# Six dense products of a graph network: tiles written out, transposes one tile ahead, bias added by VectorE

## The reference

```python
h_raw = x @ W.T + b                                   # layer 0, and x @ mag_w.T + mag_b, one column
hidden = x @ Win.T + b_in                             # layer 1
adjustment = jax.nn.relu(hidden @ W1.T + b1) @ W2.T + b2
h = (x @ W).reshape(N, HEADS, HEAD_DIM)               # layer 2, no bias
return x @ m                                          # layer 3, rotations, no bias
```

## Time and profile before

| what | us |
|---|---|
| median of three runs | 10083.64 |
| lowest and highest | 10081.59, 10103.02 |
| the profiled execution's own time | 10127.57 |
| its span, from the first to the last instruction | 10125.8 |
| the six stretches of `project` in it, together | 658.36 |
| mean granted TensorE clock, share of full speed | 0.745 |

### The profile page before, as it was taken

How to read it: one execution, slowest core, us unless ns; L and a number is a source line. 1 busy time by engine, 2 the same in 40 slices (tenths; PEclk the granted TensorE clock), 3 DMA queues, 4 the chain that set the end, 5 groups by cost and what they waited for, 6 DMA issues and landing times. The chain is left out here.

```text
span 10125.8 us, 178077 instructions
## 1 busy us (share of the span) xinstructions
PE 5548.0 (55%) x58295; PEld 4432.9 (44%) x58413; DVE 5392.1 (53%) x12231; ACT 1374.6 (14%) x3130; POOL 4357.0 (43%) x3974
## 2 busy tenths in 40 slices
PE   0001100578775725556677777777767777635552
PEld 0000000467775414333566656666566664323331
DVE  7993000355554434454566645666456663257766
ACT  0000000122211001111112111111011111112210
POOL 6887777200000035530565615656165660046630
PEclk9999555688777555556899988999889996555555
DMA  0000000000000023321555325553255530033320
GB/s 22 3 1 1 1 1 1 0 0 0 0 0 23 2 72 99 99 81 57 159 166 161 98 73 156 166 161 94 79 156 166 161 89 6 5 86 97 97 75 13
DMA packets 707863, 691.02 MB, mean 68 GB/s; under 512 B 234780, under 2 KB 588646, under 8 KB 707456
## 3 DMA queue, kind: packets, MB, share of 16 engines
q0 software_dynamic: 227328, 446.06, 16.5%
q1 hardware_dynamic: 480136, 239.99, 8.5%
HBM read 765.51 MB, written 77.58 MB: 83 GB/s over the span
## 5 line engine op out<-in xcount | busy, mean ns | idle before, releaser
L1632 POOL DMA_INDIRECT kvring<-kvtab,oth x1776 | 1900.9, 1070 | 1421.0 <-issue 711.8
L1001 POOL DMA_INDIRECT e_hg<-htab,oth_d x992 | 993.1, 1001 | 3029.0 <-issue 2597.1
L1683 PE MATMUL ea_pss<-ea_qb,ea_kT 128*128 128x128 f32 x7104 | 1146.0, 297 | 7.9 <-issue 7.6
L1683 PEld LDWEIGHTS ea_pss<-ea_qb,ea_kT 128*128 128x128 f32 x7104 | 1056.7, 213 | 37.8 <-issue 10.6
L1767 DVE TENSOR_REDUCE ea_sc<-ea_pss 128x64 f32<-128x1024 f32 x444 | 543.6, 1224 | 729.5 <-remote 613.1
L1694 PE MATMUL ea_psg<-ea_mix,kvring 128*64 128x64 f32 x14208 | 668.9, 231 | 406.8 <-issue 320.0
L1128 PE MATMUL e_psg<-e_Em,e_hg 128*32 128x32 f32 x15872 | 567.7, 245 | 465.3 <-issue 421.8
L1694 PEld LDWEIGHTS ea_psg<-ea_mix,kvring 128*64 128x64 f32 x14208 | 548.2, 140 | 557.1 <-issue 521.4
L1727 ACT ACTIVATE ea_kT<-ea_pst 128x512 f32<-128x512 f32 x888 | 481.9, 594 | 2260.5 <-remote 1596.5
L1128 PEld LDWEIGHTS e_psg<-e_Em,e_hg 128*32 128x32 f32 x15872 | 435.8, 146 | 634.1 <-issue 539.3
L1680 PE MATMUL ea_pss<-mrow,ea_mk 128*128 128x256 bf16 x1776 | 526.3, 296 | 318.3 <-ACT ea_kT L1727 298.0
(11 more groups left out here) (518 smaller groups left out, 10345.1 us busy)
## 6 DMA issues: line engine op xcount, KB each, us to landing
ea_qb<-qtab SPq DMA_DIRECT2D x1776, 64.0 KB
qtab<-at_qst SPq DMA_DIRECT2D x75, 512.0 KB, 3.3
kvring<-kvtab,oth POOLq DMA_INDIRECT x1776
e_stack<-ohtab SPq DMA_DIRECT2D x744, 32.0 KB
kvtab<-at_kvst SPq DMA_DIRECT2D x75, 256.0 KB, 2.7
e_hg<-htab,oth_d POOLq DMA_INDIRECT x992
ea_mk<-mtab SPq DMA_DIRECT2D x444, 3.0 KB
htab<-Hd SPq DMA_DIRECT2D x2, 3200.0 KB, 11.9
```

Source lines behind the costliest of these rows:

```text
L1001: pool.indirect_dma_start(out=hg[:, b % RING, u, :], out_offset=None, in_=htab, in_offset=bass.IndirectOffsetOnAxis(ap=oth[:, b * 4 + u:b ...
L1632: pool.indirect_dma_start(out=kv[:, b % R, u, :], out_offset=None, in_=kvtab, in_offset=bass.IndirectOffsetOnAxis(ap=oth[:, b * QB + u:b * ...
L1683: mm = pe.matmul(ps_s[r % 2][:, u, k * 2 * HN:(k + 1) * 2 * HN], kT[:, r % 2, u, k, :], qb[:, r, u, :], start=False, stop=True, skip_group ...
```

## The change

`project` is written anew and takes one weight function, one list of targets for a tile, a bias tile of 128 partitions and the function of the copy:

- there is no loop any more; the 25 tiles are written out on each engine;
- `xs` is gone: PE transposes from the source itself;
- PE transposes tile t + 1 before it multiplies tile t; `xT` has three slots, `psx` two, `pso` four;
- the copy from `psx` to `xT` is made by ScalarE (it was VectorE), and VectorE empties `pso` (it was ScalarE);
- the bias matmuls are gone: VectorE adds the bias as it empties `pso`. The bias is loaded as a broadcast to 128 partitions;
- the extra column of `p0` is the 257th column of the same matmul, and VectorE writes it out with a second instruction;
- Relu between `mlp1` and `mlp2` is done by ScalarE when it copies the transposed tiles of `mlp2`, no longer at the end of `mlp1`.

The core of the diff (the old loops, quoted above by the program, are left out):

```diff
-def project(nc, tag, K, src, pieces, store=None, extra=None):
+def project(nc, tag, K, src, w, dst, C=D, bias=None, entry=ACT.Copy):
...
+        xT = ctx.enter_context(nc.sbuf_tensor(f"{tag}_xT", [P, 3, 2, P], F32))
+        ps_x = [ctx.enter_context(nc.psum_tensor(f"{tag}_psx{i}", [P, 2, P], F32)) for i in range(2)]
+        ps_o = [ctx.enter_context(nc.psum_tensor(f"{tag}_pso{i}", [P, 512], F32)) for i in range(4)]
+        with phase(nc, tag, "turn xT mm out") as (block, s):
+            @block.tensor
+            def _(pe):
+                def turn(t):
+                    if t >= 2:
+                        pe.wait_ge(s["xT"], t - 1)
+                    for k in range(2):
+                        tr = pe.transpose(ps_x[t % 2][:, k, :], src[:, t, k * P:(k + 1) * P], K["ident"][:, :])
+                    tr.then_inc(s["turn"], 1)
+
+                turn(0)
+                for t in range(NT):
+                    if t + 1 < NT:
+                        turn(t + 1)
+                    pe.wait_ge(s["xT"], t + 1)
+                    if t >= 4:
+                        pe.wait_ge(s["out"], t - 3)
+                    for k in range(2):
+                        mm = pe.matmul(ps_o[t % 4][:, 0:C], xT[:, t % 3, k, :], w(k), start=(k == 0), stop=(k == 1))
+                    mm.then_inc(s["mm"], 1)
 
             @block.scalar
             def _(act):
...
+                for t in range(NT):
+                    act.wait_ge(s["turn"], t + 1)
+                    if t >= 3:
+                        act.wait_ge(s["mm"], t - 2)
+                    act.activation(xT[:, t % 3], ps_x[t % 2][:, :, :], entry).then_inc(s["xT"], 1)
 
             @block.vector
             def _(dve):
...
+                for t in range(NT):
+                    dve.wait_ge(s["mm"], t + 1)
+                    lo = 0
+                    for here in dst(t):
+                        n = here.shape[-1]
+                        if bias is None:
+                            ins = dve.tensor_copy(here, ps_o[t % 4][:, lo:lo + n])
+                        else:
+                            ins = dve.tensor_tensor(here, ps_o[t % 4][:, lo:lo + n], bias[:, lo:lo + n], ALU.add)
+                        lo += n
+                    ins.then_inc(s["out"], 1)
...
-    with nc.sbuf_tensor(f"{tag}_w", [P, 2, D], F32) as ws, nc.sbuf_tensor(f"{tag}_b", [1, D], F32) as bs:
...
+    with nc.sbuf_tensor(f"{tag}_w", [P, 2, D], F32) as ws, nc.sbuf_tensor(f"{tag}_b", [P, D], F32) as bs:
+        load(nc, tag + "l", [(ws[:, :, :], w.rearrange("(k p) n -> p k n", p=P)), (bs[:, :], b.partition_broadcast(P))])
+        project(nc, tag, K, src, lambda k: ws[:, k, :], lambda t: [dst[:, t, :]], bias=bs, entry=entry)
```

More of the change, by code:

```diff
@@ L1390, in _ @@
             @block.scalar
             def _(act):
[L1392 to L1426, removed]
-                            if bias is not None:
-                                mm = pe.matmul(ps_o[u % 2][q][:, 0:C], K["ones"][0:1, :], bias, start=False, stop=True)
-                            if q == 0 and extra is not None:
-                                mm = pe.matmul(ps_o[u % 2][q][:, 0:C], xT[0:TYPES, u, 2, :], extra, start=False, stop=True)
-                        mm.then_inc(s["mm"], 1)
@@ L1433, in _ @@
+                for t in range(NT):
[3 more added lines that the diff above has]
+                    act.activation(xT[:, t % 3], ps_x[t % 2][:, :, :], entry).then_inc(s["xT"], 1)
             @block.vector
             def _(dve):
-                dve.sem_inc(s["xT"], 1)
-                with dve.Fori(0, NT // U) as i:
-                    for u in range(U):
-                        t = i * U + u
-                        dve.wait_ge(s["turn"], t + U + 1)
-                        if extra is not None:
-                            dve.tensor_copy(xT[0:TYPES, u, 2, :], ps_x[u % 2][0:TYPES, 2, :])
-                        dve.tensor_copy(xT[:, u, 0:2, :], ps_x[u % 2][:, 0:2, :]).then_inc(s["xT"], 1)
@@ L1444, in project @@
-            if store is not None:
-                @block.sync
-                def _(sp):
-                    with sp.Fori(0, NT // U) as i:
-                        for u in range(U):
-                            t = i * U + u
-                            to, slot = store(t, u)
-                            sp.wait_ge(s["out"], t + 3)
-                            sp.dma_start(to, slot).then_inc(st[u], 16)
-                        for u in range(U):
-                            sp.wait_ge(st[u], i * 16 + 16)
-                            sp.sem_inc(s["free"], 1)
+                for t in range(NT):
[9 more added lines that the diff above has]
+                    ins.then_inc(s["out"], 1)
@@ L2175, in program @@
         rows = lambda w: w.rearrange("(k p) n -> p k n", p=P)
-        one = lambda v: v.rearrange("(a n) -> a n", a=1)
         flat = lambda v: v.rearrange("l n -> (l n)")
@@ L2214, in program @@
                     (K["w0"][:, :, 0:D], rows(io["L0_WT"])), (K["w0"][:, :, D:D + 1], io["L0_mag_w"].rearrange("a (k p) -> p k a", p=P)),
-                    (K["b0"][:, 0:D], one(io["L0_b"])), (K["b0"][:, D:D + 1], one(io["L0_mag_b"])),
+                    (K["b0"][:, 0:D], wide(io["L0_b"])), (K["b0"][:, D:D + 1], wide(io["L0_mag_b"])),
                     (K["att0"][:, :, :].rearrange("p a d -> p (a d)"), wide(io["L0_attn_w"].rearrange("a n -> (a n)")))])
```

33 lines of the change are left out of this document (10 added, 23 removed).

## The result

The changed kernel takes 9614.74 us, the median of four executions (9610.43 to 9620.06); the kernel before, beside it on the same chip, 10082.99 (10081.59 to 10103.02). The ratio is 0.9532, with a 95% interval of 0.9520 to 0.9544: 468 us less, where the sum had 474 and the forecast was 9609.

A forecast was written before the change was run, and what follows sets the result against it. Six products run alone between barriers, PE stopping in each tile at half clock. Each becomes 5.5 + 24.15 + 0.69 = 30.3 us; with loads 184.2 instead of 658.4, so 474 off 10083.64 gives 9609 us, range 9573 to 9680.

The forecast's parts named there:

- the sum: Six products and their loads: 184.2 us where they took 658.4, a gain of 474 us.
- the period 1.07: Each tile of the changed products at full clock: 0.21 us of transposes plus 0.86 of matmuls, 1.07 us.
- The stall at the start: Start of each product: first matmuls 1.17 us after the first transposes, of which 0.3 us is a stall.
- The rise, taken at 5.5 us: In each product the granted clock goes from 0.50 to 1.00 after 5.5 us, as in the attention tables.
- a rise after 13 us: Far end for the clock, from the attention update: all products rise after 13 us, 33.8 us per product.
- Slack: Each tile: ScalarE's copy to xT ends about 0.3 us before PE needs it at full clock.
- The swinging clock: Rival, 8 in 100: PE stops briefly in each tile and the clock comes and goes; gain 404, 9680 us.
- each of these has PE stopping in every tile: Argument against the clock never rising: the stretches held at 0.50 had PE stops in every tile.
- The bias matmuls go, 25 x 1.15 = 29 us in each: Four products with bias: 29 us saved in each by taking the bias matmuls off PE.
- the rival that the clock stays low: Rival, 7 in 100: granted clock 0.50 throughout the products, 328 us in all plus 2; 9755 us.
- Code that is fetched too slowly: Rival, 1 in 100: PE waits for written-out code from memory; at 2.5 instructions per us, 10145 us.
- The overlap being absent: Rival, 1 in 100: PE waits for the copy in each tile, 73 us per product, gain 218, 9866 us.

The follow-up runs named there:

- copy_in_4: The changed kernel with ScalarE's copy to xT cut into 4 instructions; 7922.36 us, 8401.79 for the kernel before beside it.
- copy_in_16: The changed kernel with ScalarE's copy to xT cut into 16 instructions of 16 columns; 7973.62 us, 8401.79 for the kernel before beside it.
- bias_matmul: The changed kernel with the bias again a one-row product on PE, VectorE only copying; 8125.25 us, 8401.79 for the kernel before beside it.
- bias_ident: The changed kernel with the bias put in by a 128-row identity matmul instead of VectorE's add; 9716.27 us, 10147.35 for the kernel before beside it.
- after_again: The changed kernel timed once more, unedited, on a faster chip; 7923.37 us, 8405.65 for the kernel before beside it.
- not_ahead: The changed kernel with PE transposing tile t directly ahead of its own matmuls, not tile t + 1; 8044.27 us, 8401.79 for the kernel before beside it.
- loop_ahead: The changed kernel with a loop and the xs ring back, transposes still one tile ahead; 9678.77 us, 10151.03 for the kernel before beside it.

## Why the prediction was right, and where its reasons were not

**The sum.** It had 182.2 us for the six products and 2 for the loads; they measured 184.3 and 1.35. The terms, one by one: the period 1.07 was 1.085, which is 22.57 x 0.015 x 6 = 2.0 us, all of the difference. The stall at the start (1.16 us to the first matmuls where the sum had 1.17, of which 0.3 idle) held. The rise, taken at 5.5 us, came after 3.7 to 6.3, 5.5 in the mean. The tail (0.69) held. The first product's one-column add took 0.148 us (asked for: 0 to 0.42). Each of the four loads took 0.2 to 0.7 us longer from its issue to the product's start, 1.35 together; wg2's load, which the change leaves as it is, was 1.4 us shorter in this execution, so a load's own spread is as large. The gain of the stretches, 474.1, is the 474 of the sum, and the medians give 468 within the 21 us over which before's own runs spread. One sum in the prediction is slightly off: with a rise after 13 us a product takes 13 + 19.07 x 1.07 + 0.69 = 34.1 us and not 33.8, so that end of the costs is 9636 and not 9634, which moves nothing else.

**Slack.** I had 0.3 us between the end of the copy to xT and PE's need; the trace of win has 4509.21 - 4508.82 = 0.39 from the end of the copy to the weight load that uses it (copy_in_4 agrees that there is some). The swinging clock, priced on the slack being gone, did not come in copy_in_16, where it was gone.

**The clock.** That it would rise was right, and so was its size. The reason was put as "each of these has PE stopping in every tile". For wg2 and pr that stands, more sharply than I could know: a stop of 0.54 or 0.55 us kept it down, 0.47 did not. (In before it was 0.52, and I had overlooked the 1.0 us at each turn of the loop.) For the four products with bias it was not needed: with PE never waiting, three of them stayed at 0.50 as long as the bias was a one-row product (bias_matmul), and with the same columns in 128 rows they rose (bias_ident). The trace of before couldn't separate the two, since every product with bias also had the stop; I took the cause that all six shared. That the clock would rise followed from this reason only in part; that the bias left PE, which the forecast counted as time alone, was needed as well, and there the right number owes something to luck. sums_to_nodes, the row that I held against the rise, has one-row products where I saw only brief stops.

The Trainium skill (TensorE: Matmul & The Clock Gate, What you observe) puts the doubling about 4 us into sustained matmuls; the six products here had 3.7 to 6.3, so the rows of the attention tables were the better guide for this execution. In after_again it was 3.2 to 5.8 us, 4.3 in the mean, nearer to the page. Its failure mode for loops that go round PSUM banks (same page, A second HAM failure mode: psum-queue depth-cycling) did not show: four banks in turn, and 1.00 from the rise to the end, in copy_in_16 too.

**The part prices.** "The bias matmuls go, 25 x 1.15 = 29 us in each" was the price at the lower clock with everything else left as it was. Put back into the changed kernel they cost 87.9 - 30.3 = 57.6 us in win, since the clock goes with them. Likewise the transposes ahead were priced by the 0.52 us; taking them back costs 302.1 - 182 = 120 us with the bias on VectorE, and 534.5 - 373.5 = 161 with it on PE, of which 39 are p0's lucky rise in bias_matmul; without it both are about 120. The total was right because it was worked out as a whole from a loop of the new form, and not from the sum of the parts. Those who forecast only one half of this change from my text would have been off: the rival that the clock stays low was given 7 in 100, and the change without its bias half met it in three of six products (bias_matmul).

**The other rivals.** Code that is fetched too slowly: PE took 12 instructions per 1.085 us without a stop. The overlap being absent: not_ahead measured what that costs, but with a clock that rises anyway: 50 us per product and not 73. Another stage moved by over 20 us only in the profiled executions, by 42 us, which the medians don't show.

## What to carry to other kernels

When TensorE runs for tens of microseconds at the lower clock, look at what stands in each tile of its loop before costing the tile's instructions: a stop of half a microsecond in three, or one-row products, was worth a factor of two on everything else. Price a change of form by a loop of the same form elsewhere in the trace, since the parts do not add. And the transposes ahead, the bias on another engine and the copy to xT on ScalarE do all of it: writing the tiles out was not needed (loop_ahead).

## What the runs showed of the hardware

- Stops that differed by 0.06 to 0.08 us per tile went with different levels of the clock: with 0.47 us in 2.97 it rose after 5 to 17 us (eight products), later and less evenly than the 3.2 to 6.3 of the changed kernel, and with 0.54 in 3.04 and 0.55 in 3.05 it stayed at 0.50 for 60 to 77 us (twelve products). In before, 0.52 in 3.02 together with 1.0 us in every fifth tile stayed at 0.50 for 82 us. What the chip counts was not measured.
- Once the clock was up, much larger idle shares did not lower it: PE at 28.57 of 39.00 us and at 31.64 of 43.00, stops of 0.47 us in 1.83 each.
- One-row f32 products (256 columns) kept a PE that waited for no engine at 0.50 for 88 us; 128-row ones of the same columns did not. Next to the one-row products the weight loads had 0.65 us of idle time that no engine explains, and whether the rows or this time count was not separated.
- The same program took 8402 to 8406 us on two chips and 10083 to 10151 elsewhere, while the changed kernel's six stretches took 180.7 us on one of the two and 184.3 elsewhere. The difference lies in other stages, and in the one shown here in idle time that no engine explains. The gather of the segment sums in the changed kernel, first on the slower kind and then on the faster (groups by line, columns as on the page):

```profile
L1001 POOL DMA_INDIRECT e_hg<-htab,oth_d x992 | 997.5, 1005 | 2687.7 <-issue 2268.7 <-PE e_psg L1131 418.6 <-DMA e_hg<-htab,oth_d 0.3
```

```profile
L1001 POOL DMA_INDIRECT e_hg<-htab,oth_d x992 | 1017.7, 1026 | 1496.7 <-issue 1448.0 <-PE e_psg L1131 48.7
```

Why the chips differ stays open. For this change it meant that a saving in microseconds carried over from one to the other, and a ratio did not (0.9532 against 0.9429).
